# Attention's exponentials kept batch by batch: the layout of a ring buffer changed, and with it who hops through memory

## What is computed

```python
xr = x.reshape(B, C, HW).transpose(0, 2, 1).reshape(B, HW, R, d).transpose(0, 2, 1, 3)   # R = 32 heads, d = 8
qkv = jnp.einsum('brnd,ed->brne', xr, w_qkv) + b_qkv
q, k, v = jnp.split(qkv, 3, axis=-1)
attn = jnp.einsum('brnd,brmd->brnm', q, k)
attn = jax.nn.softmax(attn, axis=0)            # over the 8 batches
out = jnp.einsum('brnm,brmd->brnd', attn, v)
```

## Time and profile before

| | us |
|---|---|
| median of 3 executions | 600.87 (597.69 to 601.31) |
| the profiled execution, its own time | 600.21 |
| its span, first to last instruction | 598.2 |
| VectorE busy in the span | 481.1 (80%) |
| POOL busy | 387.7 (65%) |
| TensorE busy | 504.8 (84%) |
| ScalarE busy | 328.3 (55%) |

### The profile page before, as it was taken

The page is one execution under the profiler, slowest core; times in us unless marked ns, Lnnn a source line. Parts: engine busy times, 40 slices in busy tenths (PEclk is TensorE's granted clock), DMA queues, the critical chain, the costliest instruction groups (busy, mean ns, idle before and its releaser), DMA issues.

```text
span 598.2 us, 13058 instructions
## 1 busy us (share of the span) xinstructions
PE 504.8 (84%) x4610; PEld 308.1 (52%) x4611; DVE 481.1 (80%) x876; ACT 328.3 (55%) x709; POOL 387.7 (65%) x243
## 2 busy tenths in 40 slices
PE   3999687877877778777777877799999999999996
PEld 1554354444444444444444444468986656656665
DVE  5658967999999999999999999978777873333455
ACT  3624674676676766767667676624433533333341
POOL 3200483999899998999999899923105267766640
PEclk9998895999899999999999899999999999999999
DMA  7130257244243332332433320000013223322276
GB/s 225 37 110 1 85 167 253 81 124 130 78 112 84 94 105 73 112 98 80 106 88 93 96 78 2 2 1 1 2 55 101 71 75 107 99 87 90 83 290 211
DMA packets 34288, 56.62 MB, mean 95 GB/s; under 512 B 8541, under 2 KB 21494, under 8 KB 34102
## 3 DMA queue, kind: packets, MB, share of 16 engines
q1 hardware_dynamic: 28950, 43.95, 24.8%
q0 software_dynamic: 3744, 10.39, 5.6%
q10 hardware_dynamic: 1536, 1.51, 0.8%
HBM read 38.43 MB, written 17.40 MB: 93 GB/s over the span
## 4 chain that ended last, share of the span: by engine, by line
PE 37%; POOL 29%; DVE 17%; issue 10%; ACT 3%; DMA 3%; POOLq 0%; SPq 0%; ACTq 0%; DVEq 0%
POOL e_ring L459 29%; PE ps L1890 12%; PE ps L1911 6%; DVE m_bf L1042 4%; DVE x_hat L1049 4%; PE ps L1693 2%; PE ps L1820 2%; DVE stats L865 2%; PE ps L1879 2%; ACT e_ring L644 1%; PE ps L1900 1%; PE ps L1590 1%; PE ps L1621 1%; PE ps L1839 1%; PE ps L1767 1%
## 5 line engine op out<-in xcount | busy, mean ns | idle before, releaser
L459 POOL TENSOR_TENSOR e_ring<-e_ring,x_hat 128x1024 f32<-128x1024 f32 (+1 forms) x127 | 269.8, 2127 | 30.7 <-ACT x_hat L655 18.5
L644 ACT ACTIVATE e_ring<-ps 128x1024 f32<-128x1024 f32 x128 | 131.1, 1025 | 89.7 <-PE ps L1693 89.5
L1042 DVE TENSOR_REDUCE m_bf<-ps 128x128 bf16<-128x1024 f32 x128 | 154.9, 1211 | 4.2 <-PE ps L1684 4.2
L1049 DVE TENSOR_REDUCE x_hat<-e_ring 128x128 f32<-128x1024 f32 x128 | 154.5, 1207 | 3.2 <-ACT e_ring L644 3.2
L1693 PE MATMUL ps<-m_bf,ident_neg 128*128 128x512 bf16 x256 | 82.2, 404 | 61.7 <-DVE m_bf L1042 61.5
L1712 PE MATMUL ps<-e_ring,v_slot 128*32 128x128 f32 x2048 | 86.5, 286 | 1.1 <-POOL e_ring L459 0.6
L1684 PE MATMUL ps<-q_stack,k_stack 72*128 72x128 bf16 x1024 | 83.4, 227 | 3.9 <-DMA k_stack<-qk_parts 3.9
L1712 PEld LDWEIGHTS ps<-e_ring,v_slot 128*32 128x32 f32 x2048 | 50.4, 110 | 58.0 <-issue 51.1
L1684 PEld LDWEIGHTS ps<-q_stack,k_stack 72*128 72x128 bf16 x1024 | 61.9, 101 | 32.0 <-issue 25.8
L1890 PE MATMUL ps<-w_sb,e_ring 128*128 x156 | 74.0, 598 | 1.3 <-ACT e_ring L744 0.8
L477 POOL DMA_INDIRECT e_ring<-token_rows,slot_x x39 | 37.7, 966 | 43.2 <-DVE slot_y L1331 29.5
(11 more groups left out here) (237 smaller groups left out, 674.2 us busy)
## 6 DMA issues: line engine op xcount, KB each, us to landing
q_stack<-qk_parts SPq DMA_DIRECT2D x32, 288.0 KB
k_stack<-qk_parts SPq DMA_DIRECT2D x32, 288.0 KB
w_sb<-in_w13T_dram SPq DMA_DIRECT2D x16, 256.0 KB, 7.6
qk_parts<-e_ring SPq DMA_DIRECT2D x8, 384.0 KB, 3.4
qk_parts<-scratch SPq DMA_DIRECT2D x2, 1536.0 KB, 19.7
x_res<-in_x_dram SPq DMA_DIRECT2D x8, 256.0 KB, 3.9
w_sb<-in_w2T_dram SPq DMA_DIRECT2D x8, 256.0 KB, 7.5
work<-pair_rows SPq DMA_DIRECT2D x8, 256.0 KB, 4.7
```

The source lines that it names most:

```text
L459: nc.gpsimd.tensor_tensor(ev, ev, view(x_hat, CH + (u % RS) * P, [[0, quads], [1, P], [0, 2]]), ALU.mult).then_inc(norm_done, 1)
L644: nc.scalar.activation(e_ring[:, u % ER, :].rearrange("p (q n k) -> p q n k", q=BQ, k=2), view(ps, 2 * (v % SLOT) * CH, [[2 * P, BQ], [1, ...
L1042: nc.vector.tensor_reduce(m_bf[:, u % 2], view(ps, 2 * (v % SLOT) * CH, [[1, P], [P, B]]), AX, ALU.max).then_inc(max_done, 1)
L1049: nc.vector.tensor_reduce(s_sum[:, u % 2], by_position(e_ring[:, u % ER, :]), AXY, ALU.add).then_inc(sum_done, 1)
```

## The change

The slot of `e_ring` holds batch after batch, as PSUM does: word `128 b + n` is query n of batch b. The exponential reads and writes one run; the sum reads 8 words 128 words (512 bytes) apart for each query; the multiplications take the 128 words of the inverse as one run, repeated per batch; the product reads words side by side. Number, size and order of the instructions, the semaphores and all buffers stay the same.

```diff
@@ -9,7 +9,6 @@
                       out):
     fp32, bf16 = mybir.dt.float32, mybir.dt.bfloat16
     ALU, ACT, AX = mybir.AluOpType, mybir.ActivationFunctionType, mybir.AxisListType.X
-    AXY = mybir.AxisListType.XY
 
 
     B, C, SIDE = x.shape[0], x.shape[1], x.shape[2]
@@ -456,7 +455,7 @@
             def weights(U, u, quads=BQ):
                 pool.wait_ge(r_done, U + 1)
                 ev = e_ring[:, u % ER, 0:quads * 2 * P]
-                nc.gpsimd.tensor_tensor(ev, ev, view(x_hat, CH + (u % RS) * P, [[0, quads], [1, P], [0, 2]]), ALU.mult
+                nc.gpsimd.tensor_tensor(ev, ev, view(x_hat, CH + (u % RS) * P, [[0, 2 * quads], [1, P]]), ALU.mult
                                         ).then_inc(norm_done, 1)
 
             with pool.Fori(0, NG - 1) as g:
@@ -641,8 +640,7 @@
 
                     for s in range(2):
                         act.wait_ge(parts_out[s], 16 * NCH)
-                nc.scalar.activation(e_ring[:, u % ER, :].rearrange("p (q n k) -> p q n k", q=BQ, k=2),
-                                     view(ps, 2 * (v % SLOT) * CH, [[2 * P, BQ], [1, P], [P, 2]]), ACT.Exp).then_inc(exp_done, 1)
+                nc.scalar.activation(e_ring[:, u % ER, :], score_banks(v), ACT.Exp).then_inc(exp_done, 1)
 
             def logarithm(U, u):
                 act.wait_ge(sum_done, U + 1)
@@ -1031,10 +1029,6 @@
             for n in range(2, 2 * H * NCH):
                 qk_tile(n)
 
-            def by_position(ap):
-
-                return ap.rearrange("p (q n k) -> p n q k", q=BQ, k=2)
-
             def maximum(U, v, u):
                 dve.wait_ge(scores_done, U + 1)
                 if later_than(U, 2):
@@ -1046,12 +1040,12 @@
                 dve.wait_ge(exp_done, U + 1)
                 if later_than(U, 2):
                     dve.wait_ge(ln_done, U - 1)
-                nc.vector.tensor_reduce(s_sum[:, u % 2], by_position(e_ring[:, u % ER, :]), AXY, ALU.add).then_inc(sum_done, 1)
+                nc.vector.tensor_reduce(s_sum[:, u % 2], view(e_ring, (u % ER) * UW, [[1, P], [P, B]]), AX, ALU.add).then_inc(sum_done, 1)
 
             def normalise_last(U, first):
                 dve.wait_ge(r_done, U + 1)
                 ev = e_ring[:, U % ER, first * 2 * P:UW]
-                nc.vector.tensor_tensor(ev, ev, view(x_hat, CH + (U % RS) * P, [[0, BQ - first], [1, P], [0, 2]]), ALU.mult
+                nc.vector.tensor_tensor(ev, ev, view(x_hat, CH + (U % RS) * P, [[0, 2 * (BQ - first)], [1, P]]), ALU.mult
                                         ).then_inc(norm_last, 1)
 
             def add_last(half):
@@ -1711,7 +1705,7 @@
                 for b in range(B):
                     last = nc.tensor.matmul(ps[32 * (b % 4):32 * (b % 4) + 32, 6, (b // 4) * N + nh * P:(b // 4) * N + (nh + 1) * P],
                                             v_slot[:, b * H + mh, i, :],
-                                            view(e_ring, (u % ER) * UW + (b // 2) * (2 * P) + b % 2, [[2, P]]),
+                                            view(e_ring, (u % ER) * UW + b * P, [[1, P]]),
                                             start=(u == 0 and b < 4), stop=(u == UPG - 1), skip_group_check=True)
                 last.then_inc(pv_done, 1)
 
```

## The result

The changed kernel takes 693.5 us (median of 3 executions, 690.4 to 693.7) against 600.9 before: 1.154 times as long, interval 1.146 to 1.162. The profiled execution took 693.53 us with a span of 691.5 us, 93.3 us more than the span of before. The forecast was 689 us, in a range of 650 to 742.

What follows compares the result with a forecast made beforehand. VectorE's maximum and sum were taken to bound the attention step at 2.257 us. The sum's hops added 89 us, all other edits nothing: 600.2 + 89 = 689 us, range 650 to 742.

Steps and rivals of the forecast that it cites:

- What bounds the step: Attention step: VectorE's maximum and sum, 1.13 us each, set 2.257 us; POOL follows with 0.10 us to spare.
- The price of the hop: Sum (line 1049), hopping 512 bytes at every word: 0.68 ns a word, 0.70 us a sum, 89 us over 128 sums.
- two unlike rows: SBUF reads behind the sum's price: VectorE's correlations' masked copy, 0.46 ns a word; ScalarE's turned copy of weights, 0.97.
- The free hop: Rival 1, the sum: hopping costs nothing; 600 us, or 614 if POOL's operand takes 2343 ns; chance 0.12.
- 2343 plus the 0.02 that POOL leaves between two: POOL's multiplications: plain-operand upper bound 2343 ns plus gap, paid only where the step is shorter than about 2.36 us.
- The whole second slot: Rival 2, the sum: each hop doubles a word's 1.04 ns; sum gains 1.06 us, kernel 136 us, 736 us; chance 0.13.
- the third rival: TensorE's clock falls and its loop becomes the bound: at worst 715 us; chance 0.07 with all else.
- The 0.2 us of waits: Third rival: waits around TensorE's 2.85 us at the lower clock level add some 0.2 us, 26 us more.
- What was put under cover: Exponential (-46 to 0 ns, taken as 0), POOL's multiplications (2135 to 2343 ns) and product: no effect beneath VectorE's step.
- its upper bound: POOL's multiplication with a plain operand, 1024 words: at most 2343 ns, from 2135 x 1274 / 1161.
- What was to be seen: Signs: sum's row about 1.9 us, maximum's 1.21, no VectorE holes, POOL idle some 0.6 us before each multiplication.
- The step of 2.96 us: Attention step after the change: 2.257 + 0.70 = 2.96 us, with VectorE still the bound.

## Why the prediction was right

- *What bounds the step.* That VectorE and not POOL sets it was read from spacing, not from the chain. Confirmed twice over: a longer sum carries through whole, and under the longer sum a shorter multiplication moves nothing. One reading on the way was wrong: the page's chain of before names TensorE most (37%), not POOL (29%); POOL leads by line, and in the attention's part of the chain.
- *The price of the hop.* The term was 1024 x 0.68 ns x 128 = 89 us; it measured 0.71 ns a word and 93.3 us. The total was low by that difference, under 1%. That the size came out so near was luck in part. The value came from the middle of two unlike rows, 0.71, moved to 0.68 by a weight that no row gave, and happens to lie between their errors: the correlations' copy gave 0.46 ns at 64 bytes, where the sum itself pays (1.82 - 1.13) / 1024 = 0.67; ScalarE's copy gave 0.97. The copy has a second operand and a hundred words; why it pays less was not tried.
- *The rivals.* The free hop is refuted for this pattern and shown for two others, with 8 bytes or two places. Its price was mis-sized, though: I put 13 us on POOL as the bound, it costs 4 to 6. What failed in it is "2343 plus the 0.02 that POOL leaves between two" against a step of 2.257: plain multiplications overlap by 0.04 us, the heads' additions belong into VectorE's mean, and POOL's delay is paid once at the end of the stage, not as a longer step of VectorE. The whole second slot (1.06 us more a sum) is out; the dearest hop measured, 16 bytes, adds 0.80.
- *The clock.* It fell as the third rival feared (mean 0.971 to 0.829) and cost nothing, by the reason given there: a step of TensorE's work at the lower level (granted 0.50) took 2.85 us and fits into 3.0. The 0.2 us of waits that the third rival put on top came from no row, and no such wait was seen.
- *What was put under cover.* The exponential gained nothing (1024 ns), nor did the product: 287 ns in the run with the sum back in pairs, where the clock is as before (0.969), against 286. Its 351 ns in the changed kernel go with the lower clock: with the sum alone changed, the old product took 344. POOL's row passed its upper bound by a little, 2362 ns by form against 2343; it had 94.0 / 126 = 0.75 us to wait, where 0.6 was said.
- *What was to be seen.* The step of 2.96 us is 2.99 to 3.03. That "the sum's row goes from 1207 to about 1.9 us while the maximum's stays at 1.21" is true of single instructions early and late in the stage; the rows' means, 2258 and 1531 ns, contain time in which the instruction in front was still at work.

## What to carry to other kernels

When a layout is changed for one reader, look at every reader's innermost steps, and first at the one on the engine that sets the pace: here four engines had new patterns and a single one cost 93 us. In a VectorE reduction of fp32 words from SBUF, let words that are read in turn lie side by side in pairs, or 8 bytes apart: for 1024 words both took 1.13 us, where 16 bytes between all words took 1.93 and 512 bytes 1.86 to 1.88. With pairs of neighbours, hops of 1 KiB between the pairs were free (the same 1.13 us); words 8 bytes apart were tried without a far hop. And price an instruction by the distance between starts, or ends, of a full engine, not by the mean of its row.

No version was tried that beats both kernels: the sum of the kernel before shows no price for its hops, and its step is two VectorE instructions of 1.13 us, which none of these runs shortens.

## What was not expected of the hardware

- A sum over words 8 bytes apart costs what neighbours cost (1.13 us for 1024 words), one over words 16 bytes apart 1.93 us; alternating between two places 2 KiB apart is nearly free (1.15), going round four is not (1.88).
- The maximum hops 512 bytes at every word too, in PSUM, and takes 1.13 us from start to start beside every one of these sums. So in these runs a hop of 512 bytes at every word costs a sum in SBUF about 0.73 us, while the maximum with that hop in PSUM takes no longer than a sum without a price.
- POOL's multiplication takes 2362 to 2395 ns by its row when its second operand is a plain run and 2134 to 2138 when each word of it is read twice in a row, whether the sum beside it hops or not.
- At the end of the stage VectorE's first normalisation, of 512 words, took 1155 ns before and 4727 with POOL late, in the run with POOL's operand alone. The code lets it wait for the inverse alone, the last of which ended at 387.39 us; it ended itself at 391.35, behind POOL's last multiplication (390.80). The earlier trace rows show the like for line 957's first copy. The reason was not tried.
- Two VectorE instructions in a row overlap by 0.08 us in the records of the kernel before (1.21 us long, 1.13 apart). Behind a sum that pays for hops of 512 bytes or 1 KiB the recorded starts can run ahead of the work by about 1 us, while the ends stay true; with hops of 16 and 64 bytes the maximum's row stays at 1220 ns, so there they don't. Why they drift is open.
